# A three-layer cross network on one core: the second tile's data loaded in two parts, its products five steps later, and GpSimd's first work in another order

## The reference

```python
e = stack([tbl_f[ids[:, f]] for f in range(39)], axis=1)      # (1024, 39, 16), x0
xk = x0
for W in (f0, f1, f2):                                        # (39*39,128), (128*39,128), (128*39,128)
    z = einsum('bfd,bgd->bfgd', x0, xk).reshape(b, f * g, d)
    cur = einsum('bpd,pm->bmd', z, W);  outs.append(cur);  xk = cur
z = sum(concatenate(outs, axis=1), axis=-1)                   # (1024, 384)
h = maximum(concatenate([z, dense_ctx], 1) @ W_top1 + b_top1, 0)
y = maximum(h @ W_top2 + b_top2, 0) @ W_top3                  # (1024, 1)
```

## Time and profile before

| | us |
|---|---|
| median of 3 runs | 1273.34 |
| lowest, highest | 1273.22, 1273.6 |
| the profiled execution | 1272.27 |
| its span, from the first to the last instruction | 1270.5 |
| PE busy | 1231.2 (97%) |
| DVE busy | 1080.3 (85%) |
| ACT busy | 983.5 (77%) |
| POOL busy | 964.2 (76%) |

### The profile page before, as it was taken

The page is one execution under the profiler, slowest core; times in us unless marked ns, Lnnn a source line. Parts: engine busy times, 40 slices in busy tenths (PEclk is TensorE's granted clock), DMA queues, the critical chain, the costliest instruction groups (busy, mean ns, idle before and its releaser), DMA issues.

```text
span 1270.5 us, 23146 instructions
## 1 busy us (share of the span) xinstructions
PE 1231.2 (97%) x6037; PEld 1014.9 (80%) x6037; DVE 1080.3 (85%) x3370; ACT 983.5 (77%) x3272; POOL 964.2 (76%) x745
## 2 busy tenths in 40 slices
PE   3699999999999999999999999999999999999998
PEld 2477787888888888888888888888888888888887
DVE  3499999789997899888997899978999789988884
ACT  2388888688886888788886788868888688877883
POOL 7588888678886788867887778877888678884562
PEclk9899999999999999999999999999999999999999
DMA  6484333133332234333233333313433233433000
GB/s 156 91 213 96 85 82 79 24 81 85 85 83 54 53 73 85 85 79 69 58 72 68 86 82 76 81 25 83 85 82 86 40 63 76 85 85 70 14 6 4
DMA packets 157671, 94.74 MB, mean 75 GB/s; under 512 B 112835, under 2 KB 120515, under 8 KB 157198
## 3 DMA queue, kind: packets, MB, share of 16 engines
q1 hardware_dynamic: 147299, 90.62, 31.3%
q0 software_dynamic: 10240, 2.64, 2.4%
HBM read 84.08 MB, written 3.87 MB: 69 GB/s over the span
## 4 chain that ended last, share of the span: by engine, by line
PE 90%; DVE 4%; issue 2%; POOL 2%; DMA 1%; ACT 1%; SPq 1%; DVEq 0%; ACTq 0%; POOLq 0%
PE pieces L836 22%; PE pieces L838 21%; PE pieces L837 21%; PE cur_bank L864 6%; PE cur_bank L820 4%; PE cur_bank L818 3%; PE cur_bank L819 3%; DVE parts L629 2%; POOL emb L382 2%; PE gx_bank L852 1%; PE gx_bank L853 1%; PE gx_bank L854 1%; PE cur_bank L890 1%; PE gx_bank L790 1%; PE cur_bank L874 1%
## 5 line engine op out<-in xcount | busy, mean ns | idle before, releaser
L453 ACT ACTIVATE parts<-pieces,x_cols 128x128 f32<-128x128 f32 x2560 | 723.4, 374 | 137.6 <-PE pieces L838 131.9
L629 DVE SCALAR_TENSOR_TENSOR parts<-pieces,x_cols,parts 128x128 f32<-128x128 f32 x2432 | 682.5, 342 | 139.0 <-PE pieces L838 117.6
L836 PE MATMUL pieces<-w_hi,cur_hi 128*128 128x512 f32 (+1 forms) x1280 | 515.3, 403 | 12.7 <-DVE parts L629 11.6
L838 PE MATMUL pieces<-w_hi,cur_lo 128*128 128x512 f32 (+1 forms) x1280 | 498.4, 389 | 0.0
L837 PE MATMUL pieces<-w_lo,cur_hi 128*128 128x512 f32 (+1 forms) x1280 | 498.4, 389 | 0.0
L391 POOL TENSOR_TENSOR parts<-parts 128x1024 f32<-128x1024 f32 x127 | 305.3, 2404 | 170.3 <-DVE parts L629 167.5
L382 POOL DMA_INDIRECT emb<-in_table,rows x320 | 318.1, 994 | 81.9 <-issue 57.8
L836 PEld LDWEIGHTS pieces<-w_hi,cur_hi 128*128 128x128 f32 x1280 | 241.5, 189 | 65.5 <-DVE parts L629 19.1
L838 PEld LDWEIGHTS pieces<-w_hi,cur_lo 128*128 128x128 f32 x1280 | 241.0, 188 | 51.6
L837 PEld LDWEIGHTS pieces<-w_lo,cur_hi 128*128 128x128 f32 x1280 | 241.4, 189 | 39.8
L494 ACT ACTIVATE pairs_hi<-pairs 128x512 fp32r<-128x512 f32 (+1 forms) x217 | 130.3, 600 | 63.8 <-DVE pairs L641 61.6
(11 more groups left out here) (98 smaller groups left out, 834.9 us busy)
## 6 DMA issues: line engine op xcount, KB each, us to landing
partners<-x_wide SPq DMA_DIRECT2D x93, 468.0 KB
x_diag<-x_split SPq DMA_DIRECT2D x512, 10.0 KB
x_end<-x_wide SPq DMA_DIRECT2D x96, 80.0 KB
x_rep<-x_wide SPq DMA_DIRECT2D x96, 78.0 KB
partners<-x_wide SPq DMA_DIRECT2D x93, 80.0 KB
emb<-in_table,rows POOLq DMA_INDIRECT x320
partners<-x_wide SPq DMA_DIRECT2D x31, 132.0 KB
x_wide<-emb SPq DMA_DIRECT2D x32, 80.0 KB, 2.3
```

The costliest lines, as they stand in the source:

```text
L453: last = nc.scalar.activation(parts[n % 2][:, 4 * i + r, :], src[:, r * H:(r + 1) * H], ACT.Copy, scale=x_cols[n // 4][:, n % 4, f:f + 1])
L629: nc.vector.scalar_tensor_tensor(acc, src[:, r * H:(r + 1) * H], x_cols[n // 4][:, n % 4, f:f + 1], acc, ALU.mult, ALU.add).then_inc(acc_d ...
L836: nc.tensor.matmul(dst[:, 0:width], hi[:, cols], w1_hi[:, ws], start=True, stop=False)
L838: nc.tensor.matmul(dst[:, 0:width], lo[:, cols], w1_hi[:, ws], start=False, stop=True).then_inc(l2d_ready if q in D_PIECES else l2a_ready, 1)
```

## The change

1. `load_partners` takes slots a to b. The first part is slots 0 to 2 (four transfers on `partners_loaded`). The rest goes as `load_late`: the three transfers of `x_end`, the slots 3 to 5 (four transfers), slot 6 (three). `make_pairs` waits for `partners_loaded` at k = 0 and for `partners_late` at k = 3. This holds for every tile but tile 0.
2. In tile 0 alone the products of tile 1 stand at the steps 8, 12, ... 32, and PE's sums five steps after each (13, ... 37). The split of `cur1_bank` comes at step 38 (ACT) and 39 (DVE).
3. POOL gathers tile 2 right behind tile 1, clears one half of `x_diag` behind that and the other behind the fold of block 1. In tile 0's blocks it folds first and gathers then.

```diff
+PARTNER_LOADS, LATE_LOADS = REP + 1, REP + 1 + REP
-S_PAIR = [3 + 4 * k for k in range(PAIRK)]
-S_SUM = [x + 7 for x in S_PAIR]
+class Steps:
+    def __init__(self, begin, lag):
+        self.pair = [begin + 4 * k for k in range(PAIRK)]
+        self.high = [x + 1 for x in self.pair]
+        self.low = [x + 2 for x in self.pair]
+        self.sum = [x + lag for x in self.pair]
+        self.x_bank = begin - 2
+        self.x_end = self.pair[FULL - 1] + 2
+        self.cur1 = self.sum[-1] + 1
+LATE = PAIRK // 2
+S_USUAL, S_BEGIN = Steps(3, 7), Steps(8, 5)
...
+            def load_partners(tile, i, a, b, loaded):
+                if tile == 2 and a == 0:
+                    sp.wait_ge(pairs_lo_ready, PAIRK)
                 sp.wait_ge(wide_stored, (tile + 1) * WIDE_STORES * 16)
...
+                    src = bass.AP(flat.tensor, flat.offset + (r + a * REP) * COLS,
+                                  [[COLS, F], [REP * COLS, b - a], [1, COLS]])
+                    sp.dma_start(partners[i % 2][r * F:(r + 1) * F, a:b, :], src).then_inc(loaded[i % 2], 16)
...
+            def load_late(tile, i):
+                load_end(tile, i)
+                load_partners(tile, i, LATE, FULL, partners_late)
...
-            load_partners(1, 1)
-            sp.wait_ge(diag_cleared, 2)
+            load_partners(1, 1, 0, LATE, partners_loaded)
+            load_late(1, 1)
...
-            for i in range(2):
-                pool.memset(x_diag[i][:].bitcast(FP32), 0.0).then_inc(diag_cleared, 1)
             find_rows(2, 2)
             for j in range(GATHERS):
                 gather(2, 2, j)
             find_rows(3, 3)
+            pool.memset(x_diag[0][:].bitcast(FP32), 0.0).then_inc(diag_cleared, 1)
...
+                    if first and i == 0:
+                        add_parts(u, n)
+                        if k == 1:
+                            pool.memset(x_diag[1][:].bitcast(FP32), 0.0).then_inc(diag_cleared, 1)
...
+                        steps = S_BEGIN if first and i == 0 else S_USUAL
+                if k == LATE:
+                    dve.wait_ge(partners_late[i % 2], (tile + i % 2) * 8 * LATE_LOADS)
```

More of the change, by code:

```diff
@@ L206, in cin_kernel @@
         partners_loaded = [sem(f"partners_loaded{i}") for i in range(2)]
+        partners_late = [sem(f"partners_late{i}") for i in range(2)]
         pairs_ready = sem("pairs_ready")
@@ L299, in load_x, with load_end @@
                 sp.dma_start(x_rep[i % 2][REP * F:P, :], first[0:SPARE, :]).then_inc(x_rep_loaded[i % 2], 16)
+            def load_end(tile, i):
+                first = x_wide[bass.ds(tile, 1), 0:F, :].rearrange("o r c -> (o r) c")
                 end = first[SPARE:SPARE + 1, :]
@@ L326, in load_diag @@
                 sp.wait_ge(x_lo_ready, split)
-                if not isinstance(tile, int) or tile > 0:
+                if isinstance(tile, int) and tile == 0:
+                    sp.wait_ge(diag_cleared, half + 1)
+                else:
                     sp.wait_ge(g_ready, used)
@@ L335, in _ @@
             load_x(0, 0)
+            load_end(0, 0)
+            sp.wait_ge(wide_stored, WIDE_STORES * 16)
             store_tile(1, 1)
@@ L433, in quad @@
                         add_last_parts()
-                    else:
+                    elif not (first and i == 0):
                         add_parts(u, n)
@@ L561, in quad @@
                         at = 4 * PIECES * i + s
-                        if more and s == S_XBANK:
+                        steps = S_BEGIN if first and i == 0 else S_USUAL
+                        if more and s == steps.x_bank:
                             copy_x_rep(tile + 1, i + 1)
-                        if more and s == S_XEND:
+                        if more and s == steps.x_end:
                             copy_x_end(tile + 1, i + 1)
-                        if more and s in S_HIGH:
-                            take_pairs_high(tile + 1, i + 1, S_HIGH.index(s))
+                        if more and s in steps.high:
+                            take_pairs_high(tile + 1, i + 1, steps.high.index(s))
                         if more and s == S_X + 1:
@@ L589, in quad @@
                                 copy_y(u - 1)
-                        if more and s == S_SUM[-1] + 1:
+                        if more and s == steps.cur1:
                             copy_cur1_hi(tile + 1, i + 1)
@@ L749, in quad @@
                                 step(u - 1, BLOCKS + n - 2)
-                        if more and s in S_PAIR:
-                            make_pairs(tile + 1, i + 1, S_PAIR.index(s))
-                        if more and s in S_LOW:
-                            take_pairs_low(tile + 1, i + 1, S_LOW.index(s))
+                        steps = S_BEGIN if first and i == 0 else S_USUAL
+                        if more and s in steps.pair:
+                            make_pairs(tile + 1, i + 1, steps.pair.index(s))
+                        if more and s in steps.low:
+                            take_pairs_low(tile + 1, i + 1, steps.low.index(s))
                         if q == Q_LOW:
@@ L760, in quad @@
                             take_x_low(tile + 1, (i + 1) % TILES)
-                        if more and s == S_SUM[-1] + 2:
+                        if more and s == steps.cur1 + 1:
                             take_cur1(tile + 1, (tile + 1) * TILE_B, i + 1)
@@ L935, in quad @@
                             transpose_x(tile + 1, (i + 1) % TILES, g_made(u, at))
-                        if more and s in S_SUM:
-                            sum_pairs(tile + 1, i + 1, S_SUM.index(s))
+                        steps = S_BEGIN if first and i == 0 else S_USUAL
+                        if more and s in steps.sum:
+                            sum_pairs(tile + 1, i + 1, steps.sum.index(s))
                         if at in G_STEP:
```

27 lines of the change are left out of this document (9 added, 18 removed).

## The result

The changed kernel takes 1261.88 us, the median of 6 runs (1261.15 to 1264.02); the kernel before took 1273.47 beside it (6 runs, 1272.4 to 1275.44). The ratio is 0.991, with a 95% interval of 0.990 to 0.9921: 11.6 us faster, where 11.1 were predicted. The profiled execution took 1262.40 us with a span of 1260.6, against 1272.27 and 1270.5: 9.9 us.

A forecast was written before the change was run, and what follows sets the result against it. PE bounds the kernel, so only tile 0's stall counts: 12.3 - 2.4 + 1.3 = 11.2, taken as 11.1, from 1272.27 gives 1261.2; the median 1.1 above is 1262.2 us, range 1260.2 to 1267.

The forecast's parts named there:

- 12.3 us lost in tile 0, all given back: PE in tile 0: 44.44 us against 32.15 dense; the 12.3 us of stall and low clock would all return.
- First part at 44 (42.2 to 45.9), asked at 47 to 48: Tile 1's first partners load: in before DVE's product at step 8, hidden by at least 1 us, likely 3.
- Late part at 56 (55.8 to 57.5), asked at about 57.6: Rest of tile 1's load: in before DVE's fourth product at step 20, cover 0.1 to 1.8 us, cost 0.
- New wait of 2.4 us at the end of tile 0: PE waits for the split of cur1_bank before tile 1 starts at 75.65: 2.4 us, bounds 1.4 and 3.5.
- 1.3 us back by piece 53: Early tile 1: DVE enters without debt, so PE's 11.37 us stretch becomes 10.05; gain 1.3, bounds 0 and 1.3.
- POOL's folds, cost 0: Folds in POOL's new order end before ACT needs them, tightest by 0.6 to 1.2 us: cost 0, bounds 0 and 3.
- Split in tiles 2 to 31: 0: Four added issues cost SP 1.7 us in each later tile, but PE waits for none of it: cost 0.
- POOL as the bound: Rival: POOL's closely spaced folds run late, costing 3 us at block 6 or 7: 1265 us, chance 0.10.
- late data: Rival: first or late part lands several us after DVE asks, PE stands about 4 us: 1267 us, chance 0.13.
- exposed issues: Rival: the split's added transfers delay PE in every tile: 1275 us if a quarter exposed, 1312 fully; slower, chance 0.03.
- The change doesn't take the wait away: Rival: DVE waited for something other than partners, so the wait only moves five steps on: 1272 us, chance 0.02.

The follow-up runs named there:

- steps-only run: The kernel before, with only the later steps and POOL's new order, loads in one part as before: 1272.32 us, ratio 0.9996.
- warm wait: The changed kernel with eight matmuls of 512 columns on PE ahead of its wait for the split of cur1_bank in tile 0: 1263.71 us.
- the one with step 6 and the late order: The changed kernel with tile 1's products at steps 6, 10, ..., x_end behind slots 3 to 5, slot 6 on its own semaphore: 1261.2 us.

## Why the prediction was right, and where not

The mechanism was the one predicted. Off were a term that the sum did not have (the clock behind the new wait), the credit for the later steps, and what the first tile's gain does to tile 3.

- *12.3 us lost in tile 0, all given back.* Right in kind: PE waits nowhere between 40.92 and 73.2, and its clock is full there. In size it is 12.0: without the new wait tile 0 takes 34.79 - 2.36 = 32.43 us, where 32.15 had been worked out. The steps-only run confirms what the earlier trace rows does not name: DVE waited for the partners, 8.97 us even when it asked five steps later.
- *First part at 44 (42.2 to 45.9), asked at 47 to 48.* It landed at 45.72, at the late end, and was asked for at 47.83.
- *Late part at 56 (55.8 to 57.5), asked at about 57.6.* 56.41 and 57.65. At 51 to 62 us the DMA share is 0.29, close to the 0.26 of the earlier trace rows. Of the two figures weighed there, 56 by the Trainium skill's rule on the number of engines ("DMA: Bandwidth & Descriptors", section "Why a DMA increments its semaphore by 16 and not by 1") and 50 by an even load, the landing agrees with the first. With `x_end` put behind them and slot 6 on its own semaphore, slots 3 to 5 land at 48.4 to 49.2 and slot 6 at 54.35 and 55.31, so what comes last are the transfers of 4 x 10 rows, `x_end` and slot 6, whose share of each delay no run separates.
- *New wait of 2.4 us at the end of tile 0.* 2.36. The loads alone, with the old steps, don't have it. The cost was sized rightly and credited wrongly: it buys nothing that shows, since at step 3 too the first part is there, if only by 0.1 us (45.83 and 45.94).
- *1.3 us back by piece 53.* Right in the profile: piece 53 starts at 87.37, and less the 1.6 of the low clock that is 85.8, against 75.65 + 10.05 = 85.7 forecast.
- *The low clock behind the new wait: not in the sum.* This is the term that failed. It costs 1.6 us in those executions that have it, by the warm wait (46.45 to 44.89). The profiled executions of the changed kernel have it, that of the kernel with POOL as before doesn't. With it, 12.3 - 2.4 + 1.3 - 1.6 = 9.6, and the first piece starts 0.2 sooner (40.92 against 41.12): 9.8 of the 9.9 measured between the two profiled executions. Part of that agreement is chance: by the starts of the pieces the 9.9 are 0.2 up to the first piece, 9.65 in tile 0 (12.0 less 2.36), -0.3 up to piece 53, +0.5 from there to piece 80 (24.35 and 23.88), which the sum did not have, and -0.2 behind it. That the median came out at 11.6, so near the 11.1 forecast, is partly luck: three of its six executions are at clock 1.0 and 1261.15 to 1261.36, what the sum says for a program with full clock, and the median of before lies 1.2 above its profiled execution. On the next occasion the same kernel gained 10.1.
- *POOL's folds, cost 0.* They ended at 54.6, 63.0, 73.0, 80.5 and 92.4 (forecast 54.5, 62.9, 73.1, 81.0, 93.0). The old order costs nothing either, so the part was free and empty. (Three more gathers lie between the fourth and the fifth fold than before; the number ahead of the fifth is the same.)
- *Split in tiles 2 to 31: 0.* No cost, as forecast; a gain that I missed in tile 3. I had worked out when its first part would be in (by 108; it was 109.3), but not when an unsplit load would be. At 117.9, as in the kernel with the split for tile 1 only, it is 2.9 us late, because DVE comes to it 11.5 us sooner than before the change and the load only 5.0. The profiled span of the kernel with the split for tile 1 only is 5.4 us above that of the changed kernel. Its five times spread over 4.8 us, and its median is not told apart (ratio 0.9926 against 0.9922).
- *Rivals.* POOL as the bound, late data and exposed issues: none showed in the changed kernel. The four added transfers overlap with the others: the last data are in at 56.41, against 55.70 before, where 2.3 us for each would have made it 65. The figure of about 2.0 us, which the prediction takes from the Trainium skill ("DMA: Bandwidth & Descriptors", section "Anatomy of one DMA"), is fitted there on transfers that GpSimd issues, and these are SP's. "The change doesn't take the wait away" is what the steps alone do.

The simplest kernel with the whole gain is the one with the loads alone, 1261.57 us; the one with step 6 and the late order has 1261.2, and the two are not told apart.

## What to carry to other kernels

When one wait hides behind a load, ask first what part of the load the first user needs; splitting the transfer gave the whole gain, while moving the user later gave 1.3 us of DVE's time and cost a wait elsewhere. After a gain at the start, look again at every transfer whose time is set by another queue: tile 3's load came 5.0 us sooner and its user 11.5, and the slack of 3.6 us was gone. And price a new wait of PE not only by its length but by the clock behind it.

## What the runs showed of the hardware

- The granted clock fell to its lower level behind a wait of PE of 2.36 us, for 3.4 us, in four of the six profiles that have this wait; the same 2.36 us had it in the changed kernel and not with POOL's old order. Matmuls of 512 columns then start 0.43 us apart instead of 0.23, so 3.4 us at 1.2 GHz cost 1.6 us. Behind longer waits it was low for 6.8 or 10.2 us.
- In four of the six profiles with a full clock throughout tile 0 and tile 1 it fell in the last tile instead, where PE's waits are 0.6 to 1.4 us long; that cost 1.5 to 1.6 (33.7 and 33.8 instead of 32.2) or 2.6 us (34.8).
- This, and not the change, goes with most of the spread from 1260 to 1268 us. Over the changed kernel and the experiments that lose nothing in tile 0, the executions with a mean clock of 1.0 take 1259.94 to 1261.36 us, those at 0.999 take 1261.57 to 1263.43, those at 0.997 take 1262.86 to 1265.45, and the two at 0.996 take 1264.87 and 1267.78.
- With eight matmuls in the wait at the end of tile 0 the clock stayed full behind it in both profiles that have them. Whether they do the same in the last tile is not shown: three profiles with them have a full clock there, but so have seven of eleven without. Neither lowered a median here.
- Three programs stood 7 to 10 us in their first 55 us on PE, DVE and ACT at once, in four runs on two occasions, while POOL's gathers went on every 1.25 us, though their code there equals that of programs that don't. The DMA traffic was unchanged in the one whose twin was run. In the other two, which stood between 38 and 48 us, SP's issues were slower too (three of `x_end` in 3.05 and 2.38 us instead of 1.92) and the DMA share was lower (0.45 and 0.49 instead of 0.91 from 43 to 48 us) than in the changed kernel. One differed from its twin only in six matmuls of the last tile. A kernel compared with another needs its first stretch looked at before its time is put down to the edit.
